# Letting the 32 scatters of a batch go out without a wait for landing between parts of four

## The reference

```python
top_w, top_idx = jax.lax.top_k(probs, 8)              # 160 experts, 8 for each token
h1 = jax.nn.silu(jnp.einsum('th,eih->eti', x, w_gate))
h1w = h1 * combine.T[:, :, None]
routed = jnp.einsum('eti,ehi->th', h1w, w_down)
```

## Time and profile before

| | |
|---|---|
| runs of the kernel | 1480.31 and 1482.79 us, median 1481.55 |
| span of the profiled execution | 1367.7 us |
| median less span | 113.85 us |
| stage 1, by the trace | from the start to about 797 us |
| stage 2, by the trace | from about 795 us to the end |
| scatters of the first batch issued | from 155.8 us |
| scatters of the last batch issued | 834.9 to 914.2 us |

### The profile page before, as it was taken

The page is one execution under the profiler, slowest core; times in us unless marked ns, Lnnn a source line. Parts: engine busy times, 40 slices in busy tenths (PEclk is TensorE's granted clock), DMA queues, the critical chain, the costliest instruction groups (busy, mean ns, idle before and its releaser), DMA issues. The chain is left out here.

```text
span 1367.7 us, 22150 instructions
## 1 busy us (share of the span) xinstructions
PE 1160.1 (85%) x6688; PEld 657.2 (48%) x6688; DVE 936.1 (68%) x2795; ACT 615.4 (45%) x1294; POOL 550.4 (40%) x606
## 2 busy tenths in 40 slices
PE   4999999998998999999989979799687977967811
PEld 2434344433443433434434347588476765756600
DVE  4546877868868858768758646070859669678784
ACT  1424234223233323233232247677686776766611
POOL 0000361351440550541622512344656565656565
PEclk9999999999999999999999999899798988989955
DMA  9952013013002012112139358876565746746522
GB/s 295 301 238 83 28 42 97 22 40 94 29 33 92 33 45 77 39 39 77 37 114 288 129 179 256 230 236 212 152 193 185 234 146 197 227 153 209 165 64 59
DMA packets 155818, 183.59 MB, mean 134 GB/s; under 512 B 16621, under 2 KB 104237, under 8 KB 155078
## 3 DMA queue, kind: packets, MB, share of 16 engines
q1 hardware_dynamic: 139334, 148.83, 33.8%
q0 software_dynamic: 16384, 33.59, 8.5%
HBM read 83.79 MB, written 98.57 MB: 133 GB/s over the span
## 5 line engine op out<-in xcount | busy, mean ns | idle before, releaser
L1201 POOL DMA_INDIRECT y<-y_rows,idxy x256 | 259.6, 1014 | 186.1 <-DMA y<-y_rows,idxy 81.7
L1165 POOL DMA_INDIRECT rows<-xn,idx x256 | 252.2, 985 | 88.0 <-issue 84.9
L1029 ACT ACTIVATE hs<-GY 128x512 f32<-128x512 f32 x176 | 104.9, 597 | 333.4 <-PE GY L780 333.3
L796 PE MATMUL ACC<-hs,wff 128*128 128x512 f32 x352 | 188.4, 624 | 0.0
L780 PE MATMUL GY<-xn0T,wff 128*128 128x512 f32 x352 | 185.8, 610 | 0.0
L1725 DVE SCALAR_TENSOR_TENSOR V<-y,w8all,V 128x128 f32<-128x128 f32 x232 | 82.5, 356 | 114.8 <-PE V L933 99.0
L1145 POOL TENSOR_TENSOR ppause<-neg_half 128x1 f32<-128x1 f32 x64 | 13.8, 215 | 342.7 <-DVE idx L1495 231.5
L830 PE MATMUL U<-ident,xg 128*128 128x128 f32 x576 | 98.2, 296 | 53.8 <-ACT xT L1045 50.4
L1552 DVE TENSOR_TENSOR hs<-hs,B 128x512 f32<-128x512 f32 x96 | 65.8, 685 | 65.7 <-PE B L786 34.9
L830 PEld LDWEIGHTS U<-ident,xg 128*128 128x128 f32 x576 | 69.3, 150 | 78.5 <-issue 63.8
L786 PE MATMUL B<-xw,wff 128*128 128x512 f32 (+2 forms) x304 | 102.8, 612 | 1.2 <-DVE hs L1552 0.7
(11 more groups left out here) (273 smaller groups left out, 2085.8 us busy)
## 6 DMA issues: line engine op xcount, KB each, us to landing
xg<-rows SPq DMA_DIRECT2D x144, 256.0 KB
y_rows<-ys SPq DMA_DIRECT2D x144, 256.0 KB
rows<-zero SPq DMA_DIRECT2D x2, 12288.0 KB, 47.0
rows<-zero SPq DMA_DIRECT2D x6, 2048.0 KB, 9.5
wd<-in_wd SPq DMA_DIRECT2D x1, 5120.0 KB, 24.4
wff<-in_w SPq DMA_DIRECT2D x3, 1408.0 KB, 9.4
rows<-xn,idx POOLq DMA_INDIRECT x256
y<-y_rows,idxy POOLq DMA_INDIRECT x256
```

The source lines that it names most:

```text
L796: nc.tensor.matmul(ACC[:, :], w2_0[:, v, :], hs[:, v % RH, :], start=(v == 0), stop=(v == U0 - 1))\
L1029: nc.scalar.activation(hs[:, u % RH, :], G[u % 2][:, :], ACT.Silu).then_inc(sem["silu_ready"], 1)
L1165: pool.indirect_dma_start(rows, bass.IndirectOffsetOnAxis(ap=idx[:, t * 8 + k:t * 8 + k + 1], axis=0), xn1[:, t, :], None)\
L1201: pool.indirect_dma_start(y8[:, i % RG, k, :], None, y_d[0:groups * Q * P, :], bass.IndirectOffsetOnAxis(ap=idxy[:, b, t * 8 + k:t * 8 + k ...
```

## The change

The wait for landing between the parts is taken out, with the small multiplication behind it. The one ahead of the first part stays. The count of events of that semaphore in a batch goes from 8 to 1.

```diff
-    dve_link=0, pool_link=T * TOPK1 // PART,
+    dve_link=0, pool_link=1,
...
                 pool.wait_ge(*seen.next("idx_ready"))
                 waited("pool_link")
                 for part in range(T * TOPK1 // PART):
-                    if part:
-                        pool.wait_ge(sem["scattered"], seen.value("scattered", seen.count["scattered"] + 16 * PART * part))
-                        waited("pool_link")
                     for j in range(part * PART, (part + 1) * PART):
                         t, k = divmod(j, TOPK1)
                         pool.indirect_dma_start(rows, ...)
```

## The result

The changed kernel takes 1679.47 us (median of 2 runs, 1677.19 to 1681.76) where the kernel before takes 1481.55: 1.135 of it, with a 95% interval from 1.127 to 1.143. The forecast was 1483.0, between 1477 and 1489. The change costs 198 us, and none of the four cases had a price of that size.

The account below looks back on a forecast made before the run. PE was taken as the bound (busy 85% of the span), with POOL early in stage 1. Stage 1 0, seam 0, stage 2 +1.5 us made the span 1369.2; with 113.85 around it, 1483.0 us, range 1477 to 1489.

Parts of the forecast that it names:

- the four cases: Whole kernel: the forecast 1483.0 us (chance 0.73), relief 1478 (0.11), SP's transfers crowded out 1493.5 (0.11), no unbroken stream 1481.5 (0.05).
- The sum's first term: Whole kernel: the profiled span of 1367.7 us becomes 1369.2; with 113.85 us around it, 1483.05 us.
- Worth on the path: 0: Stage 1: 12.5 us a batch removed from POOL gain 0, since DVE's row releases POOL's next instruction anyway.
- The step's own list of covers: Stage 1: if DVE came early by 4.41 us or more, the cover would be gone and 12.5 us would count.
- the +1.5 of stage 2: Stage 2: sixteen scatters move before 883 us, adding 2.8 to 3.6 us of DMA time there; 1.5 us taken as cost.
- the third rival: POOL's scatters: POOL must stop whenever more than a few are out, so they end as late as now; 1481.5 us, chance 0.05.
- The first two rivals: Stage 2: relief after 883 us gives up to 3.6 us, 1478 (0.11); SP's transfers crowded out, +12 us, 1493.5 (0.11).
- the second: Stage 2, 834 to 880 us: scatters crowd out SP's transfers, seventeen groups pay 0.70 us each, 1493.5 us; chance 0.11.
- Its list of what would prove it wrong: PE's waits (834 to 883 us) growing over some 6 us, POOL pausing inside most batches, or DVE's instructions getting longer.

Follow-up runs that it names:

- the half-rows run: The changed kernel with 64 of the 128 rows in each scatter: 1378.29 us beside 1369.83 us of the kernel before, ratio 1.004.

## Why the prediction was wrong

**The sum's first term failed.** "With 113.85 us around it" took the distance between the median and the profiled span as fixed time around the span. Every other execution here has 1.8 us there. A span on a loud chip holds the rest, 112.8 us more than the span shown: 48.7 ahead of the eighth batch and 64.1 behind its start, by the table. That was no small book-keeping slip. It was the one row that said that the trace and the times are not of the same level, and that an effect worth 8% of the time is missing from the trace. Had it been asked what fills it, the range would have had to be wide.

**"Worth on the path: 0" failed on the loud chips.** The step read the wait as idle time of an engine that is early. There it is also the gap in which the other engines go on. Taking it out costs 12 to 28 us a batch instead of 0 (118.4 against 106.7 for the fourth, 130.2 against 102.0 for the first). The step's own list of covers named DVE getting earlier as what could undo it. What happened is the reverse: DVE, PE and ACT got later.

**On a quiet chip the step holds, and so do most others.** The changed kernel's windows of the same stretch, and those of stage 2 that answer to the earlier trace rows:

```profile
170.00:196.00 26.00, 25.67 (x156) 10.76 (x145) 19.87 (x83) 7.28 (x25) 19.80 (x21) 1.00 0.16 54
...
834.00:851.00 17.00, 16.63 (x183) 12.30 (x181) 12.69 (x77) 13.64 (x27) 8.04 (x9) 1.00 0.93 295
851.00:867.00 16.00, 8.69 (x76) 6.32 (x76) 0.00 (x0) 5.48 (x12) 12.04 (x14) 0.79 1.00 199
867.00:883.00 16.00, 13.84 (x135) 9.86 (x133) 0.00 (x0) 11.37 (x28) 10.53 (x11) 0.99 0.89 308
883.00:899.00 16.00, 12.93 (x106) 9.38 (x106) 11.57 (x12) 12.73 (x23) 0.00 (x0) 0.79 0.63 182
899.00:915.00 16.00, 16.00 (x155) 14.12 (x154) 15.41 (x33) 13.04 (x25) 0.00 (x0) 1.00 0.79 247
```

and POOL's timeline there, where it waits for DVE, where it pauses, and at the first gather:

```profile
508.79 1.04 POOL L1138 TENSOR_TENSOR rs<-rs,neg_half 128x4 f32<-128x4 f32 x1 [16.78 <-DVE rs L1236]
...
842.99 0.96 POOL L1162 DMA_INDIRECT rows<-xn,idx  x1 [6.82 <-issue]
...
933.24 0.98 POOL L1198 DMA_INDIRECT y<-y_rows,idxy  x1 [52.66 <-DMA y_rows<-ys]
```

DVE's row releases the inverse square root after 16.78 us (about 17 was forecast). The batches are as long as before, and the gather starts within 0.1 us of 933.2. PE's stall at the small table grows by 0.94 us (9.63 to 8.69 busy), and the DMA share there rises to 1.00. By 915 us PE has done 655 matmul instructions of these windows where the earlier trace rows have 675, a group of 20 less, which is about the delay that was forecast. The span is 1366.7 against 1367.7: the +1.5 of stage 2 was given back, or is smaller than the runs' scatter. The pause after the 226th DMA is 6.82 us instead of 4.95. It isn't that more are out, as the third rival held possible: in both kernels it comes behind the second scatter of its batch, and the one after the 113th is 3.10 us in both. The first two rivals didn't come about there. On the loud chips none of the three gives the loss: in stage 1 PE's standstills have a DMA share of 0.16, in stage 2 of 0.24 to 0.31, where the second needs full DMA engines.

Its list of what would prove it wrong named DVE's instructions getting longer beside an unbroken stream. That was the right place with the wrong sign to look for: they keep their length (936.6 us in all) and start later.

**What stays open.** The runs narrow the cause to indirect DMAs issued by POOL with too little gap between them, on some chips. What the engines share with them is not shown. One candidate is the supply of instructions. The Trainium skill, Runtime: NRT & Kernel Launch, Instruction fetch mechanics, says that an engine's sequencer streams its instructions in through a DMA queue of its own while it executes. An undersupplied stream would look like waits for issue that set in late, after what was already there had been used. The result run speaks against it. Its profile lists two instruction queues; their last packet before the standstill comes at 172 to 174 us, and from 174 to 216 us the DMA queues list POOL's alone:

```profile
q0 software_dynamic: 609, 1.25, 8.9%
```

```profile
174.00:202.00 28.00, 9.38 (x17) 2.78 (x16) 3.22 (x17) 0.78 (x4) 17.30 (x18) 0.51 0.13 45
202.00:216.00 14.00, 14.00 (x57) 5.05 (x56) 6.67 (x27) 2.78 (x10) 0.00 (x0) 0.65 0.00 0
```

PE runs 17 matmuls in the 28 us of the standstill and then 57 in 14 us, and not one packet of instructions came in between. The changed kernel's runs on the two other loud chips list none from 174 to 212 us either. Unless they come by a way that the profile doesn't list, they lay ready all the time, and something else held them back. Another candidate is the recording itself: every execution of these series comes with a span and a granted clock, so none shows the kernel without the profiler's records, and no run tells whether these have a part in it. Open too are why plain DMAs do no harm (no run has indirect DMAs to neighbouring rows), whether the rows or the DMAs of a scatter count, which pace is the limit, and why the chips differ.

## What to carry to other kernels

Before costing anything, compare the profiled span with the times: a gap far above the 1.8 us of the runs here means that the trace isn't of executions like those that were timed, and then its slack and covers hold only for the level it was taken at. A wait on an engine that is early may be a throttle for the others, so ask of every wait that is taken out what will now be issued back to back. For indirect DMAs on POOL, put a short gap behind each one (0.65 us here) rather than a long wait behind every few; it cost nothing on a quiet chip (1371.09 us beside 1367.82) and gained 3.7% on a loud one.

## What the runs showed of the hardware

- The same program takes 1368 to 1370 us on two chips and 1480 to 1495 us on three (medians); each level held through all runs of a series on its chip (28, 21 and 19 of the kernel before on three of them). No chip was used in two series.
- 32 indirect DMAs of POOL at 1.26 us each bring PE, DVE and ACT almost to a halt from 9 to 14 us after the first until a few us after the last, on the loud chips alone. The load is the same on a quiet chip, 54 GB/s and a DMA share of 0.16. PE then takes an instruction every 2.1 to 2.8 us, in steps of about 0.70 us, and its granted clock falls to the lower level, 0.50.
- No packet of an instruction queue comes in from 174 to 216 us, while PE goes from 17 matmuls in 28 us to 57 in 14 us.
- One gap of 3.1 us in the stream lets PE go on (2.6 us after its start in the result run), and some 9 to 14 us after the stream's return it stands again.
- 32 plain DMAs of the same bytes, 0.54 us each, have no such effect.
- POOL pauses after the 113th and the 226th DMA of 128 rows, in indirect and plain form: for 2.87 to 4.02 us, and for 4.77 to 6.82 us. With 64 rows in each (the half-rows run) neither pause is there, and one of 3.57 us comes after the 128th.
